# GpSimd's indirect sends of a sequence-mixing and mixture-of-experts layer are made to wait for progress of the other engines

## The reference

```
x = layernorm(x + mixer(x))
x = layernorm(x + moe(x))

def mixer(x):
    xs, z = split(x @ W_in.T)                 # 512 each
    xc = silu(causal depthwise conv of 4 taps(xs) + conv_b)
    xp = xc @ W_x.T;  dt = xp[..., :32]
    a  = softplus(dt @ W_dt.T + b_dt)
    return (xc * a * silu(z)) @ W_out.T + x

def moe(x):                                   # 16 experts, I = 128
    scores = sigmoid(x @ gate_w.T)
    # 2 of 4 groups by the sum of their two best, then top 4 of 16 experts
    topk_w = 2.5 * scores[topk] / sum(scores[topk])
    y = sum over the 4 picked experts of topk_w * down(silu(gate(x)) * up(x))
    shared = silu(x @ Ws_g.T) * (x @ Ws_u.T) @ Ws_d.T
    return x + y + shared
```

## Time and profile before

| | before |
|---|---|
| time, median of 3 runs | 692.46 us (690.92 to 692.55) |
| the profiled execution's own time | 690.66 us |
| its span in the trace | 688.9 us |
| mean granted TensorE clock | 0.911 |
| TensorE busy | 80% |
| VectorE busy | 61% |
| ScalarE busy | 55% |
| GpSimd busy | 47% |
| DMA, mean over the span | 161 GB/s |

### The profile page before, as it was taken

How to read it: one execution, slowest core, us unless ns; L and a number is a source line. 1 busy time by engine, 2 the same in 40 slices (tenths; PEclk the granted TensorE clock), 3 DMA queues, 4 the chain that set the end, 5 groups by cost and what they waited for, 6 DMA issues and landing times.

```text
span 688.9 us, 11736 instructions
## 1 busy us (share of the span) xinstructions
PE 552.7 (80%) x3143; PEld 465.4 (68%) x3143; DVE 417.3 (61%) x1123; ACT 379.0 (55%) x969; POOL 323.1 (47%) x361
## 2 busy tenths in 40 slices
PE   6897999999999988766291788697697797796694
PEld 5684767777777776555180787697696686686584
DVE  5794989888888896644250363322222355565586
ACT  4777676767676764605120555554555455455454
POOL 3402123676767667573537345453453453453420
PEclk9999999999999999998596799898898898898898
DMA  8963031424242312494244277453353775775297
GB/s 212 277 216 131 31 124 49 151 79 150 80 152 78 122 69 95 154 383 154 91 146 145 83 224 230 135 169 116 115 163 117 240 217 177 248 227 180 97 351 263
DMA packets 69094, 110.92 MB, mean 161 GB/s; under 512 B 11204, under 2 KB 52421, under 8 KB 68520
## 3 DMA queue, kind: packets, MB, share of 16 engines
q1 hardware_dynamic: 55800, 74.23, 34.4%
q0 software_dynamic: 12672, 35.67, 14.3%
q10 hardware_dynamic: 560, 0.27, 0.1%
HBM read 61.50 MB, written 49.69 MB: 161 GB/s over the span
## 4 chain that ended last, share of the span: by engine, by line
PE 45%; another core or an unknown queue 17%; ACT 13%; DVE 12%; issue 11%; DMA 1%; ACTq 0%; SPq 0%; DVEq 0%
PE psum L737 4%; PE psum L803 4%; PE psum L738 4%; PE psum L739 4%; PE psum L1021 4%; PE psum L881 3%; PE psum L1011 3%; PE psum L1013 3%; PE psum L1012 3%; DVE xc L1491 3%; PE psum L995 2%; PE psum L1035 2%; ACT y_out L1341 2%; PE psum L1037 1%
## 5 line engine op out<-in xcount | busy, mean ns | idle before, releaser
L669 POOL DMA_INDIRECT x_buf<-row,row_id x128 | 128.5, 1004 | 75.2 <-issue 37.5
L2101 DVE TENSOR_TENSOR e_act<-g_act,psum 128x512 f32<-128x512 f32 x36 | 24.8, 688 | 137.6 <-ACT g_act L1326 109.2
L1011 PE MATMUL psum<-ew_gu_hi,t_hi 128*128 x286 | 91.7, 321 | 0.4 <-issue 0.4
L1326 ACT ACTIVATE g_act<-psum 128x512 f32<-128x512 f32 x36 | 21.8, 606 | 124.9 <-remote 100.2
L661 POOL TENSOR_TENSOR m<-xc,zs 128x512 f32<-128x512 f32 x32 | 41.5, 1317 | 102.2 <-DVE shift L1569 57.4
L1012 PE MATMUL psum<-ew_gu_lo,t_hi 128*128 x286 | 87.5, 306 | 0.0
L726 POOL DMA_INDIRECT y_buf<-y_out,y_ids x56 | 55.3, 987 | 68.4 <-ACT y_out L1341 46.0
L1013 PE MATMUL psum<-ew_gu_hi,t_lo 128*128 x286 | 87.3, 305 | 0.0
L1491 DVE SCALAR_TENSOR_TENSOR xc<-psum,cw_taps,xc 128x511 f32<-128x511 f32 (+2 forms) x96 | 70.7, 738 | 6.7 <-ACT halo_x L1147 5.3
L1021 PE MATMUL psum<-ident,e_act 128*128 128x128 f32 x143 | 27.4, 324 | 52.2 <-DVE e_act L2101 52.1
L1011 PEld LDWEIGHTS psum<-ew_gu_hi,t_hi 128*128 128x128 f32 x286 | 62.9, 220 | 0.6 <-issue 0.5
(11 more groups left out here) (263 smaller groups left out, 1469.4 us busy)
## 6 DMA issues: line engine op xcount, KB each, us to landing
tiles_in<-x_buf SPq DMA_DIRECT2D x143, 144.0 KB
y_pair<-y_buf SPq DMA_DIRECT2D x20, 512.0 KB
y_in<-y_buf SPq DMA_DIRECT2D x12, 512.0 KB, 8.0
xT<-in_x_T SPq DMA_DIRECT2D x8, 512.0 KB
xtok<-in_x_tok SPq DMA_DIRECT2D x8, 512.0 KB
gu_hi_buf<-w_hi_now SPq DMA_DIRECT2D x8, 512.0 KB, 2.6
x_buf<-pad_row SPq DMA_DIRECT2D x17, 144.0 KB
raw_gu<-in_wg_T SPq DMA_DIRECT2D x16, 128.0 KB, 3.4
```

The lines of the kernel that those rows point to most:

```text
L669: nc.gpsimd.indirect_dma_start(out=x_buf, out_offset=bass.IndirectOffsetOnAxis(ap=row_id[t % ROWS][:, b, k:k + 1], axis=0), in_=row[t % RO ...
L1011: pe.matmul(o, t_hi[par][:, k, r], w_hi, start=k == 0, stop=False)
```

## The change

In the last token tile each block's four sends get a wait of their own, for a named semaphore of another engine; the order of the sends stays. In the quads the four sends of a quad are split in two pairs. The first pair waits for `e_mul`, the second for `a_l`, to reach `quads_begun(q)`, which is q + 5 for the first five quads, q + 4 up to quad 17 and q + 3 after that, at most 36. Nothing is removed, and no other engine's program changes.

```diff
+            def send_behind(t, b, name, n):
+                at_least_alone(pool, name, n)
+                send(t, range(b, b + 1))
+
+            def quads_begun(q):
+                return min(q + (5 if q < 5 else 4 if q < NQ // 2 else 3), NQ)
...
-                send(t - 3, range(2, SUB))
-                send(t - 2)
-                send(t - 1)
-                send(t)
+                send(t - 3, range(2, 3))
+                send_behind(t - 3, 3, "res_done", 2 * (t - 2) + 1)
+                send_behind(t - 2, 0, "y_done", PAIRS * t + 1)
+                send_behind(t - 2, 1, "h_done", KS * (t - 1) + 1)
+                send_behind(t - 2, 2, "ln_in", 2 * (t + 1))
+                send_behind(t - 2, 3, "norm_ready", t + 1)
+                send_behind(t - 1, 0, "x1T_l", KD * (t + 1))
+                send_behind(t - 1, 1, "t_l", 2 * KD)
+                send_behind(t - 1, 2, "e_mul", 1)
+                send_behind(t - 1, 3, "a_l", 1)
+                send_behind(t, 0, "res_done", 2 * (t + 1))
+                send_behind(t, 1, "a_l", 2)
+                send_behind(t, 2, "a_l", 3)
+                send_behind(t, 3, "e_mul", 4)
...
                 for i in range(tiles_of(q)):
+                    if i % 2 == 0:
+                        at_least_alone(pool, "a_l" if i else "e_mul", quads_begun(q))
                     nc.gpsimd.indirect_dma_start(
```

## The result

The changed kernel took 665.93 us (median of 4 runs, 661.79 to 670.31) against 692.50 us for the kernel before: a ratio of 0.965, 95% interval 0.958 to 0.971. The forecast was 656.7 us, with 603 to 694 as its range. A session is a group of runs made one after another on one chip: in three of the sessions of experiments the kernel before took 687 to 698 us as here, in five it took 548 to 549 us, and the traces taken in those five show no "remote" wait before `g_act`, so the two kinds are called stalled and unstalled and each number stands beside the kernel before of its own session.

A forecast was written before the change was run, and what follows sets the result against it. TensorE's semaphores, held behind unbroken rows of GpSimd's sends, were taken to bound the kernel. Terms -21.3, -17.4 and +2.9 sum to -35.8, from 690.66 to 654.9; with 1.8 for the median, 656.7 us, range 603 to 694.

The forecast's parts named there:

- What bounds the kernel: Expert stage: TensorE's semaphores due a few us into an unbroken row of GpSimd sends come 1.1 to 2.7 us behind it.
- To the layernorm: Last tile: four sends wait behind the layernorm, so the row in front ends earlier; gain 5.1 us, bounds 0 and 10.2.
- First quads: Last tile's waits remove the row of 20 sends; quad 5's `g_act` comes at 381.2 instead of 402.47: -21.3 us.
- Quads 5 to 35: 30 quads at 7.5 us plus 10.3 for two rows of eight: 235.3 against 252.7, so -17.4 us.
- The ring of a held quad: Silu and product 1.29, send start 0.77, row of four 4.86, release 1.1: 8.0 us; 6.2 if let through.
- The held bound: Quads 5 to 35 if every quad is held: 30 x 8.0 + 10.3 = 250.3 us.
- The end: The last quad's sends wait for `e_mul` 36 and `a_l` 36 and end later: +2.9 us, or 0.
- B: Rival: the pause between the pairs lets everything out, a quad takes 6.2 us; 612.3 us in all, chance 0.25.
- C: Rival: sends and stalls both wait for a third thing, perhaps traffic, so nothing is gained; 692.5 us, chance 0.09.
- D: Rival: every gate_up ends inside a row and release takes 1.50 us, 8.42 a quad; slower, 705.7 us, chance 0.18.
- Three signs of being right: "Remote" idle before `g_act` far below 100.2 us; from quad 5 a `g_act` every 7.5 us; quads' clock nearer to 0.99.
- one sign of being wrong: In the changed profile, a row of GpSimd's sends longer than eight would speak against the forecast.

The follow-up runs named there:

- the `gu_mm` kernel: Changed kernel with a quad's four sends waiting for `gu_mm` instead of `e_mul` and `a_l`: 636.34 us stalled (kernel before 698.15), 548.44 us unstalled (before 548.90).

## Why the prediction was right, and where it was not

**What bounds the kernel**: right for the stalled sessions, to which the forecast belonged, and wrong for the others, which nothing in the trace of before gave away. There the expert stage is bound by TensorE alone, and the change does nothing. The prediction did not know of the two kinds; it holds because the result was measured in the kind that its rows came from.

**To the layernorm**: 5.1 us were forecast (bounds 0 and 10.2), 8.1 came. The group in front of the layernorm was four sends shorter, as forecast, and it also began 2.7 us earlier (286.02 against 288.74), for a reason that wasn't looked into.

**First quads**: `g_act` was forecast at 326.4, 339.6 and 357.2 and came at 324.6, 334.2 and 352.6; quad 5 at 381.2, it came at 377.9. The term was -21.3 and measured -24.6. The way there was another, so part of the hit is luck. The first `g_act` was to fall behind a group of four sends, and it came 1.6 us behind one of eight that had begun earlier (313.19 to 323.00). The second was to be held by a row of eight, but the sends behind `e_mul` and `a_l` made two groups of four (326.23 and 333.54), and it went through at once, 0.7 us into the second. Quads 2 to 5 took 6.5, 12.2 and 6.7 us and not 8.0 each. The cause was put wrongly too: the text gave it to the last tile's waits ("the row of 20 sends is gone"), and the run with these alone brought that row back. It is the quads' waits that keep it away.

**Quads 5 to 35**: this term failed in its size: -17.4 forecast, -8.1 measured. The ring of a held quad was worked out as 8.0 us and measured as 8.00 (64.02 us for the 8 quads from 438.60 to 502.62). The step that failed is the choice of 7.5 us a quad, which took every fourth quad or so to be let through. An increment due 2.73 us into a group of four was held in all 12 cases. The held bound gave 250.3 us for the 30 quads, 244.6 came, and the two rows of eight account for the difference: they were priced at 5.16 each above a held quad, and cost 2.8 and 2.1 (10.81 us from 403.69 to 414.50, 10.11 from 502.62 to 512.73), since in both the increment came before the group's end. The other 28 quads took 223.7 us, 7.99 each: slower ones beside longer groups and faster ones that went through, such as that from 586.5 to 591.4, cancel out.

**The end**: +2.9 forecast, +4.2 measured.

The sum was -35.8, and -28.5 came; against the two medians it is -35.8 and -26.6, as the runs of the changed kernel lie 3.8 us above its profiled execution. They lie at 662 and at 670 us, two each, and what makes the 8 us between them was not looked into.

**The rivals.** B, that the pause lets everything out, did not happen, for the reason given: `a_l` is there before the first pair is through, so there is no pause. C, that the sends do not cause the stalls, falls in its traffic form with the run without bytes, and the 18 increments that came 0.91 to 1.06 us behind a group and the 6.81 us of the `gu_mm` kernel speak against the rest; but the unstalled sessions show that the sends alone don't cause them either. D needed a release of 1.5 us behind each group; 1.0 was measured, so the 30 quads gained 8.1 us rather than nothing. Three signs of being right did not show: the "remote" idle did not fall, as 24 quads now have such a wait where 11 had one, the `g_act` rows came every 8.0 us, not 7.5, and the clock of the quads was 0.88 and 0.93 in the two windows, where it was to come nearer to 0.99. And one sign of being wrong did show: a row of sends longer than eight. There is one of 12 (286.02 to 301.22) and one of ten (504.80 to 517.40), where the pair of the next quad found its wait fulfilled and followed the eight. The split into pairs was taken to be idle, and the trace bears that out for the steady quads; in the first quads pairs of sends do stand apart, such as the one from 390.45. The kernel without it was measured only where nothing stalls, so its worth in the first quads is open, and so is the time of the quads' waits alone.

## What to carry to other kernels

Where a long group of one engine's instructions delays another engine's signals, do not ask only how long the group is, but at which point of the ring it starts: with the same four sends a quad took 8.0 us behind `e_mul` and 6.8 behind `gu_mm`, since there they lie beside the silu and the product. Work that is held back lands somewhere: pacing one producer alone brought its row of 20 back with the next producer's sends in it. And measure the kernel before again in every session: the gain was 3.5% where the kernel before took 692 us, and none where it took 549 us, there with this change and with four variants of it.

## What was not expected of the hardware

The same program took 549 us or 687 to 698 us, by the session and not by the chip. In the slower kind TensorE's increments are held beside GpSimd's indirect sends: due 2.73 to 4.23 us into a group of four they came 0.91 to 1.06 us behind its end in 18 quads of the changed kernel, due at 1.8 they came at once, and taking the sends' bytes away (139 to 79 GB/s) changed a quad from 8.00 to 7.96 us. The exceptions are unexplained: at 2.95 and at 3.57 one came at once, and in a group of eight and one of ten it came before the end. In the faster kind sends follow each other at the same 1.29 us with no increment held. Which property of a session decides this the runs don't show.
